# A fused gated cross-attention and mixture-of-experts kernel: split evictions of qh and Af, three maxima in each of steps 0 to 6, and the first PV matmuls ahead of the next scores

## The reference

```python
xn = ln(x);  cn = ln(context)
q = xn @ Wq;  k, v = split(cn @ Wkv)
k = concat(null_k, k);  v = concat(null_v, v)
sim = einsum('bhid,bhjd->bhij', q * 0.25, k)        # 16 heads, 56 x 1501
attn = softmax(where(mask, sim, -max))
out = ln(einsum('bhij,bhjd->bhid', attn, v) @ Wo)
x = x + tanh(g_xattn) * out
h = gelu(einsum('bsh,ehf->ebsf', ln(x), w1) + b1)
y = einsum('ebsf,efh->ebsh', h, w2) + b2            # of 8 experts, the one with the largest score is kept
x = x + tanh(g_ffn) * y
```

## Time and profile before

| | us |
|---|---|
| median of 3 runs (749.33 to 753.48) | 753.14 |
| the profiled execution, its time | 749.7 |
| its span, first to last instruction | 747.9 |
| PE busy | 696.9 (93%) |
| DVE busy | 570.1 (76%) |
| ACT busy | 509.6 (68%) |
| POOL busy | 388.7 (52%) |

### The profile page before, as it was taken

The page is one execution under the profiler, slowest core; times in us unless marked ns, Lnnn a source line. Parts: engine busy times, 40 slices in busy tenths (PEclk is TensorE's granted clock), DMA queues, the critical chain, the costliest instruction groups (busy, mean ns, idle before and its releaser), DMA issues.

```text
span 747.9 us, 14835 instructions
## 1 busy us (share of the span) xinstructions
PE 696.9 (93%) x5041; PEld 396.2 (53%) x5041; DVE 570.1 (76%) x1001; ACT 509.6 (68%) x650; POOL 388.7 (52%) x462
## 2 busy tenths in 40 slices
PE   3698989999989998999899989998999899899997
PEld 2454444455544544454445444544454445468886
DVE  4976878787877786878787878787878675877776
ACT  1416676767676766676767676767676767687895
POOL 6654567773727372737373737273737235656200
PEclk9759999999999999999999999999999999999999
DMA  5825091726080606060616061616121201010000
GB/s 158 176 68 56 1 124 43 123 44 85 26 84 25 84 25 84 25 81 28 74 34 82 27 75 34 81 27 79 29 43 25 42 26 57 26 27 2 12 4 14
DMA packets 73992, 40.33 MB, mean 54 GB/s; under 512 B 61309, under 2 KB 68501, under 8 KB 73957
## 3 DMA queue, kind: packets, MB, share of 16 engines
q1 hardware_dynamic: 73525, 39.77, 32.8%
q10 hardware_dynamic: 432, 0.10, 0.1%
HBM read 26.65 MB, written 0.52 MB: 36 GB/s over the span
## 4 chain that ended last, share of the span: by engine, by line
PE 68%; ACT 12%; DVE 11%; issue 5%; DMA 2%; POOL 1%; ACTq 0%; SPq 0%; DVEq 0%; POOLq 0%
PE S L1208 23%; PE A L1228 21%; PE X L1266 9%; ACT S L675 5%; ACT PP L680 4%; PE S L1365 4%; PE A L1382 3%; DVE mx L1006 3%; DVE PP L961 2%; DMA raw<-ctx_dram 2%; PE X L1382 1%; DVE st L999 1%; ACT nullrow L703 1%; PE X L1276 1%; PE A L1151 1%
## 5 line engine op out<-in xcount | busy, mean ns | idle before, releaser
L675 ACT ACTIVATE S<-S,mb 125x896 f32<-125x896 f32 x192 | 187.7, 977 | 168.8 <-PE S L1208 168.8
L961 DVE TENSOR_TENSOR PP<-S,PP 125x896 f16<-125x896 f32 x192 | 209.3, 1091 | 98.5 <-ACT PP L680 92.6
L1006 DVE TENSOR_REDUCE mx<-X 128x1 f32<-128x500 f32 x336 | 212.1, 669 | 11.7 <-PE X L1266 9.7
L1228 PE MATMUL A<-PP,z_hi 125*128 125x448 f16 x768 | 206.4, 353 | 3.5 <-ACT Af L759 3.5
L680 ACT ACTIVATE PP<-S 125x896 f16<-125x896 f32 x192 | 175.2, 912 | 4.9
L1266 PE MATMUL X<-zTh,qh 128*128 128x500 f16 x336 | 134.5, 406 | 17.9 <-DVE ql L982 11.6
L1228 PE MATMUL A<-PP,z_lo 125*128 125x448 f16 x384 | 121.7, 353 | 0.0
L1228 PEld LDWEIGHTS A<-PP,z_hi 125*128 125x128 f16 x768 | 74.5, 98 | 75.5 <-ACT Af L759 5.8
L1208 PE MATMUL S<-qh,zTh 128*128 128x448 f16 x384 | 104.6, 354 | 1.7 <-DVE PP L961 1.7
L1208 PE MATMUL S<-qh,zTl 128*128 128x448 f16 x384 | 104.0, 352 | 0.0
L1208 PE MATMUL S<-ql,zTh 128*128 128x448 f16 x384 | 104.0, 353 | 0.0
(11 more groups left out here) (202 smaller groups left out, 1185.5 us busy)
## 6 DMA issues: line engine op xcount, KB each, us to landing
raw<-ctx_dram SPq DMA_DIRECT2D x16, 750.0 KB
Rb<-r_scratch SPq DMA_DIRECT2D x16, 448.0 KB, 3.5
wst<-in_w_dram SPq DMA_DIRECT2D x16, 256.0 KB, 3.0
early<-in_Wkv_dram SPq DMA_DIRECT2D x2, 512.0 KB, 14.2
early<-in_Wq_dram SPq DMA_DIRECT2D x1, 512.0 KB, 5.6
Wo_s<-in_Wo_dram SPq DMA_DIRECT2D x1, 512.0 KB, 11.7
zTh<-z_hi SPq DMA_TRANSPOSE x32, 3.7
zTl<-z_lo SPq DMA_TRANSPOSE x32, 3.8
```

Source lines behind the costliest of these rows:

```text
L675: act.activation(s, s, ACT.Exp, bias=mb[:, p, c:c + 1]).then_inc(e_done, 1)
L961: dve.tensor_tensor(Pl[:, k, :].rearrange("p (a r) -> p a r", a=2), S[0:CK, 2 * (c % 2):2 * (c % 2) + 2, 0:HR], Ph[:, k, :].rearrange("p ( ...
L1006: dve.reduce_max(mx4[:, np_].rearrange("q k t -> q (k t)")[:, j:j + 1], X[:, j % 2, 0:KB], AX).then_inc(mx_red, 1)
L1228: ins = mm(A[:, a, 0:HR], z[:, p, c, :], q[:, k, a * HR:(a + 1) * HR], start=(c == 0 and n < 2), stop=(c == NC - 1 and n >= 4))
```

## The change

- **Maxima.** Three in each of steps 0 to 6 (before: two in step 0, three in steps 1 to 6, one in step 7), and on DVE all three reductions of a step stand ahead of its `sub`. The shifts move from steps 8 and 9 to steps 6 and 7, the statistics of a later batch all to steps 7 and 8 (before: six in step 9 and three in each of steps 0 and 1 of the next body).
- **PV first.** In each step from 1 on the first three PV matmuls of chunk c stand ahead of the scores of chunk c+2; the last three come after the second maximum. In step 10 all six stood ahead of the scores before.
- **Queries.** Their 48 matmuls move from the end of step 10 to the end of step 8. Half 0 of qh is evicted by ACT in step 9, half 1 by DVE in step 9 (new `query_hi`); the two null rows become one instruction of 896 columns on ACT, in step 10, and it waits for both ql.
- **Af.** ACT copies the first half (between the exponential and the fp16 copy of step 11), DVE the second (new `a_half`, behind the `sub` of step 11). The first PV matmul of the next batch waits for both (a_copied, a2_copied).

```diff
 # ScalarE, body
+                    if c == NC - 1 and f["main"] and f["prep"]:
+                        a_copy(b, f["tail"])
                     if exp_slot:
                         exps_hi(*ahead(b, c))
+                    if c == 7 and f["prep"]:
+                        shifts(nb, np_)
+                    if c == 9 and f["znext"] and f["main"]:
+                        act.wait_ge(sim_done, NC * b + NC)
+                        query_hi(b + 2, p, 0, X[:, 0, 0:HR])
+                    if c == 10 and f["znext"] and f["main"]:
+                        queries_null(b + 2)
-                    if c == NC - 1 and f["main"] and f["prep"]:
-                        a_copy(b, f["tail"])
 # ScalarE, a_copy
-                act.activation(Af[:, :].rearrange("d (a r) -> d a r", a=2), A[:, :, 0:HR],
-                               ACT.Copy).then_inc(a_copied, 1)
+                act.activation(Af[:, 0:HR], A[:, 0, 0:HR], ACT.Copy).then_inc(a_copied, 1)
 # VectorE
+            def query_hi(n, p):
+                dve.wait_ge(q_ready, 2 * n + 2)
+                dve.wait_ge(sim_done, NC * (n - 1))
+                ch.link(dve.tensor_scalar(qh[:, p, HR:R], X[:, 1, 0:HR], rowmask[:, 0:1], rowbias[:, 0:1], ALU.mult,
+                                          ALU.add))
+            def a_half(b, b_ge1):
+                dve.wait_ge(pv_done, NC * b + NC)
+                if b_ge1:
+                    dve.wait_ge(an_done, b)
+                dve.tensor_copy(Af[:, HR:R], A[:, 1, 0:HR]).then_inc(a2_copied, 1)
 # VectorE, body
-                        for j in MAXIMA.get(c, ())[:2]:
+                        for j in range(3 * c, min(3 * c + 3, NMX)):
                             reduce(nb, np_, j)
+                    if c == 9 and f["znext"] and f["main"]:
+                        query_hi(b + 2, p)
+                        low_half(b + 2, p, 1, X)
+                    if c == 10 and f["znext"] and f["main"]:
+                        queries(b + 2, p, 0)
                     if (f["main"] and c + 2 < NC) or (f["prep"] and c + 2 >= NC):
                         sub(*ahead(b, c))
+                    if c == NC - 1 and f["main"] and f["prep"]:
+                        a_half(b, f["tail"])
 # TensorE, body
+                    values = f["main"] and not experts
+                    if values and c > 0:
+                        pv(b, c, p, f["tail"], 0)
                     if scores:
                         sim(*ahead(b, c), p if c + 2 < NC else 1 - p)
                     for part in range(3):
                         if f["prep"]:
                             aux(b, p, c, part, f)
-                        if f["main"] and c != 10 and not experts and part < 2:
-                            pv(b, c, p, f["tail"], part)
+                        if values and c == 0 and part == 0:
+                            pv(b, c, p, f["tail"], 0)
+                        if values and part == 1:
+                            pv(b, c, p, f["tail"], 1)
                     if c == NC - 1 and f["y"]:
-                            pe.wait_ge(qlo_done, 2 * b + 5)
+                            pe.wait_ge(null_done, 2 * b + 6)
```

More of the change, by code:

```diff
@@ L311, in flags @@
                         group=b == B - 1)
-        MAXIMA = {0: (0, 1), 1: (2, 3, 4), 2: (5, 6, 7), 3: (8, 9, 10), 4: (11, 12, 13), 5: (14, 15, 16),
-                  6: (17, 18, 19), 7: (20,)}
+        STATS = {7: range(0, HC), 8: range(HC, NC)}
         STEADY = [flags(4), flags(5)]
@@ L700, in query_hi, with queries_null @@
                                scale=rowmask[:, 0:1], bias=rowbias[:, 0:1]).then_inc(qhi_done, 1)
+            def queries_null(n):
+                act.wait_ge(null_in, 16 * n)
+                act.wait_ge(qlo_done, 2 * n + 2)
+                act.activation(nullrow[0:1, :].rearrange("o (a r) -> o a r", a=2), X[0:1, :, 0:HR], ACT.Identity,
+                               scale=1.0 / W_SCALE, bias=rowbias[0:1, 0:1]).then_inc(null_done, 2)
             def null_scores(j, row):
@@ L732, in body @@
                         act.activation(b1T[:, :], A[:, 1, 0:E * FC], ACT.Copy).then_inc(b1_copied, 1)
-                    if c == 10 and f["znext"] and not queries_early:
+                    if c == 10 and not f["main"]:
                         queries(b + 2, p, 0)
@@ L977, in take_y, with queries, low_half @@
                                          ALU.add).then_inc(y_done, 2)
-            def queries(n, p, j, banks=X):
-                dve.wait_ge(null_done, 2 * n + j + 1)
+            def queries(n, p, j, banks=X, early=False):
+                if early:
+                    dve.wait_ge(null_done, 2 * n + j + 1)
+                else:
+                    dve.wait_ge(qhi_done, n + 3)
+                low_half(n, p, j, banks)
+            def low_half(n, p, j, banks):
                 dve.scalar_tensor_tensor(ql[:, p, j * HR:(j + 1) * HR], banks[:, j, 0:HR], rowmask[:, 0:1],
@@ L1012, in body @@
                     if f["prep"]:
-                        for j in MAXIMA.get(c, ())[:2]:
+                        for j in range(3 * c, min(3 * c + 3, NMX)):
                             reduce(nb, np_, j)
-                    if c == 8 and f["prep"]:
+                    if c == 6 and f["prep"]:
                         dve.wait_ge(mx_red, NMX * (nb + 1))
@@ L1021, in body @@
                                           negate=True).then_inc(mneg_done, 1)
[L1022 to L1026, removed]
+                    if c == 9 and f["znext"] and f["main"]:
[3 more added lines that the diff above has]
+                        queries(b + 2, p, 0)
+                    if c == 11 and not f["main"]:
+                        queries(b + 2, p, 1, early=True)
+                    if c in STATS and f["load"]:
+                        context_stats(b + 3, 1 - p, STATS[c], 16 * ((b - p) // 2 + 2 + p) if isinstance(b, int)
                                       else (b - p) * 8 + 32 + 16 * p)
@@ L1029, in body @@
                         sub(*ahead(b, c))
[L1030 to L1037, removed]
+                    if c == 10 and not f["main"]:
+                        queries(b + 2, p, 0, early=True)
+                    if c == NC - 1 and f["main"] and f["prep"]:
+                        a_half(b, f["tail"])
                     if f["group"]:
@@ L1269, in aux @@
                         value_step(4 + j // 2)
-                if c == 8 and not f["main"] and part == 1:
+                if c == 7 and not f["main"] and part == 0:
                     value_step(14)
                     value_step(15)
-                if c == 8 and part == 2:
+                if c == 7 and part == 1:
                     pe.wait_ge(mneg_done, nb + 1)
@@ L1281, in aux @@
                             value_step(k)
-                if c == 10 and part >= 1 and f["znext"]:
-                    queries(b + 2, p, part - 1, True)
+                if c == (8 if f["main"] else 10) and part == 2 and f["znext"]:
+                    queries(b + 2, p, 0, True)
+                    queries(b + 2, p, 1, True)
             def project(b, bank):
@@ L1298, in body @@
                     scores = f["main"] if c + 2 < NC else f["prep"]
-                    if c == 10 and f["main"]:
-                        pv(b, c, p, f["tail"], 0)
-                        pv(b, c, p, f["tail"], 1)
                     experts = f["group"] and c == NC - 1
```

26 lines of the change are left out of this document (13 added, 13 removed).

## The result

| | before | after |
|---|---|---|
| median of 3 runs, us | 753.14 | 766.15 (764.99 to 766.26) |
| after over before, 95% interval | | 1.018 (1.0145 to 1.0214) |
| the profiled execution, its time | 749.7 | 766.26 |
| its span | 747.9 | 764.5 |
| PE busy | 696.9 (93%) | 709.2 (93%) |

The change took 16 us of work off ScalarE and gave 22 to VectorE.

A forecast was written before the change was run, and what follows sets the result against it. The prediction took PE to set the time: middles +3, ends without projection +5.5 and with it +3 made +11.5 us on the profiled 749.7, 761; allowing for the median 3.4 above that execution, it forecast 762 us, range 750 to 774.

The forecast's parts named there:

- The ends: Ends without projection: first PV matmul waits for DVE's half of Af behind sub; +0.7 us in 8 bodies, +5.5.
- With the projection: Body ends with projection: first maximum waits for take_y behind DVE's half of Af; +0.5 us in 6 bodies, +3.
- The new steps 7 to 10: Steps 7 to 10 of a body: costed at nothing, statistics and shifts fitting DVE's and ACT's free time.
- The middles: Steps 1 to 6: third maximum waits for the first's reduction; step 3.15 us, +0.2 a body, 15 bodies, +3.
- the 0.46: Middle steps: time from the start of a maximum's matmul to the start of its reduction, part of a 1.19 us way.
- the prediction's lower bound: Middle steps with 0.05 us less on the third maximum's way: a body 18.6, -1.5 us in all.
- The cheap stop: Rival, middle steps: a stopped maximum's weight load goes ahead; 12 us less, 750; chance 0.2 for 749 to 756.
- Faster: Rival, middle steps: the third maximum never waits; six steps 17.4, 19 us won against 8.5 lost, 739; chance 0.1.
- The clock: Rival, ends without projection: half clock at more ends, some 1.7 us each; chance 0.2 for 767 to 774.
- its forecast: Whole kernel: 762 us predicted, with 756 to 767 given a chance of 0.5.
- its signs of being wrong: Steps 1 and 7 less than 18.5 apart, PE released at the end by ACT's half, or half clock at several ends.
- 2.8 us of VectorE's time in a middle step of 3.15: Middle steps: DVE's three reductions at about 0.6 and a sub of 1.01, so DVE is free when the maximum comes.

The follow-up runs named there:

- grouped reductions alone: Kernel before, with only three maxima in each of steps 0 to 6 and all three reductions ahead of the sub: 750.65 us, 0.9985 of before.
- null row on VectorE: Changed kernel with VectorE's Af half ahead of sub, old TensorE order in steps 1 to 6, and VectorE computing the null row in step 10: 723.39 us, 0.9614.
- half of Af first: Changed kernel with VectorE's half of Af ahead of its sub of step 11 instead of behind it: 746.69 us, 0.9928 of before.
- half first, PV behind the scores: Changed kernel with VectorE's half of Af ahead of sub and the old TensorE order in steps 1 to 6: 728.87 us, 0.9695 of before.
- Af whole on ScalarE: Changed kernel with ScalarE copying the whole of Af right behind the fp16 copy of step 11, VectorE none: 747.31 us, 0.9936 of before.
- null row later: Changed kernel with ScalarE's null row, in bodies without projection, moved from step 10 to behind the fp16 copy of step 11: 755.16 us, 1.0039 of before.
- statistics alone: Kernel before, with only the twelve statistics of a later batch moved to steps 7 and 8, none in steps 0 and 1: 751.79 us, 0.9996.
- PV behind the scores: Changed kernel with TensorE's order in steps 1 to 6 as before (scores, maximum, three PV, maximum, three PV, maximum): 751.25 us, 0.9987 of before.

## Why the prediction was right, and where it was not

**The ends: right, step by step.** From the last scores S the prediction had the exponential of step 11 at S + 6.40, VectorE's half behind the `sub`, and the first PV matmul at S + 10.44. The rows have 215.57 - 209.08 = 6.49 and 219.53 - 209.08 = 10.45, and 0.61 for the half, whose 0.60 was chosen between bounds. The ends are 0.67 longer (0.7 predicted). With the projection the first maximum came at S + 10.90 (10.88; those last scores started at 246.72), and the ends are 0.52 longer (0.5). That the place behind the `sub` is the cause is shown from both sides: the half moved, and the halving undone. The new steps 7 to 10, costed at nothing, did cost nothing: in a body without the projection TensorE stands, from the scores of step 7 to the first PV matmul of the next batch, only for the 0.63 and the 2.21.

**The middles: the mechanism right, the term too large.** Every step from 1 to 6 has the third maximum waiting for the first one's reduction, but a step is 3.115 and not 3.15, so the term of +3 was +0.6. The step of the sum that failed is the 0.46 from the start of a maximum to its reduction. It came from a maximum that had stopped itself; behind one that runs through it is 223.21 - 222.80 = 0.41. That is the 0.05 less of the prediction's lower bound.

**The cheap stop: did not happen.** In the row at 223.94 the load waits 0.43 for the reduction, and the matmul follows 0.01 later. The other bodies show the same price, with middles of 18.68 to 18.70 wherever the clock is full. The Trainium skill, "TensorE: Matmul & The Clock Gate", section "Architectural detail: the array is 16x 32x32, not 1x 128x128", says that PE's queue can pull weight loads ahead of matmuls in flight. At these stops the trace shows no load that ran ahead.

**Faster: did not happen, though the gain it spoke of exists.** Six steps in 17.4 were possible (17.5 was measured), but not in the order that the change gives TensorE.

**The clock: a rival that came true beside the forecast.** Four of eight ends were followed by half clock, +5.0 in the profiled executions that the sum did not hold. The prediction treated it as an alternative to its forecast; it adds to it. Half clock at several ends was also one of its signs of being wrong, and that sign came true although the waits that the sum was made of were there.

**The first body: not costed at all, +1.9.** 0.5 of it was there before the first scores (57.96 and 58.46), and 0.83 is work that changed sides of the cut (67.78 to the first scores of step 1 at 68.61). The rest, 0.6, is a wait in step 0 of body 0:

```profile
66.05 1.09 DVE L967 TENSOR_TENSOR PP<-S,PP 125x896 f16<-125x896 f32 x1 [1.12 <-ACT PP L681]
...
67.06 1.86 DVE L1033 TENSOR_REDUCE mx<-X 128x1 f32<-128x500 f32 x3
67.78 0.13 PEld L1298 LDWEIGHTS X<-zTh,qh 128*128 128x128 f16 x1 [1.41 <-DVE mx L1033]
```

Step 0 has a third maximum now, and its bank comes free behind the last `sub` of the body before.

Without the half clock the two executions differ by 11.6 us, where the sum was 11.5. That it fits so closely is in part luck: the middles are 2.4 below their term, and the start and the stretch behind body 14, for which the sum had nothing, make up for it. Of these the stretch behind body 14 and the 0.5 before the first scores are no effect of the change that any run shows. The distance of 762 from 766.15 says little by itself: the sum was put on the profiled execution's 749.7, which is 3.4 below the median of before; on that median it gives 764.6.

**What stays open.** The prediction reckoned 2.8 us of VectorE's time in a middle step of 3.15 and called it free. In the changed kernel it is: the reductions at 223.21 start after 0.24 of idle time. With the statistics still in steps 0 and 1 it is not, as the grouped reductions alone show. How much of the +5.0 of half clock belongs to the change is only estimated, in the last section.

## What to carry to other kernels

A copy that is halved between two engines is done when the later half is; on an engine that takes its instructions in order, the half belongs ahead of the first instruction that waits for something else. Where two matmuls share a bank, the work between them is what hides the reduction that frees it: count it in us before moving a group of matmuls, and compare it with the way from matmul to reduction to weight load (1.15 here). And when a reorder changes the time little, measure its parts one by one: here one part was worth some -17 us and another +18.

## What was not expected of the hardware

What no sum held is how often TensorE falls to half clock at the ends without the projection. The table counts it by the granted clock of each profiled execution, with the longest piece for which TensorE stands at such an end:

| kernel | longest piece, us | ends followed by half clock |
|---|---|---|
| null row on VectorE | 0.83 | 0 |
| half of Af first | 0.86 | 0 |
| half first, PV behind the scores | 0.87 | 0 |
| Af whole on ScalarE | 1.01 | 0 |
| null row later | 1.19 | 0 |
| before | 1.52 | 1 |
| grouped reductions alone | 1.52 | 4 |
| statistics alone | 1.52 | 4 |
| after | 2.21 | 4 |
| PV behind the scores | 2.21 | 6 |

Two such stretches (busy time by stretch) of the kernel with the grouped reductions alone, whose ends are those of before:

```profile
287.90:291.30 3.40, 3.40 (x11) 1.35 (x9) 2.28 (x4) 1.00 (x2) 0.00 (x0) 0.50 2.14 79
363.00:366.40 3.40, 3.40 (x10) 1.35 (x9) 1.97 (x4) 1.32 (x2) 0.00 (x0) 0.50 1.45 65
```

Ends of the same length had one such stretch in one kernel and four in another, so the length of the standing does not say by itself at which end the clock falls.

Only the profiled executions tell which ends they were, but every execution has its mean granted clock on record. The three of the changed kernel have 0.973, 0.973 and 0.971, of which the profiled one is at 0.973; of the 39 executions of the kernel before that ran beside the experiments, 29 have 0.975 to 0.978 and 10 have 0.971 or 0.973. So the four are no accident of one execution, and before is not always at one. The time at half clock can be estimated from these means as 2 x (1 - mean clock) x span: 42 us for the changed kernel and 37 on the average for before, start and end of the kernel included. Half of the difference is lost time, some 2.6 us that the change costs by the clock on the average: about half of the +5.0.

The spread from run to run follows the clock only in part. With PV behind the scores, the two executions at 0.971 and 0.972 took 748 us and the eight at 0.964 to 0.966 took 750.8 to 754.4. But executions of the kernel before took 749.38 us at 0.976 and 753.4 at 0.977, and what makes its times differ by 4 us stays open. The five kernels without half clock behind an end spread by 0.7 to 2 us. With the ends' half clock, four stretches of 1.66 to 1.7, went some 6.7 us of the changed kernel that no sum over waits shows.
